# An attention kernel: latent queries as nine fp16 products instead of three fp32 ones, and the products moved between heads

## Chip, core and metric

One Trainium2 chip, one of its cores. The metric is the device time of one execution in microseconds, the median of the runs shown, with the lowest and the highest. The profile is of one further execution.

## What is computed

A two-layer block on x of shape (8, 256, 256) with a context of (8, 1601, 64). The change touches only the first attention of 16 heads:

```
q_big = einsum("bshk,hkq->bshq", (x_norm @ Wq.T) split in heads, w_kc_q)     # 192 wide
q_big = q_big * cos_q + rotate_half(q_big) * sin_q
q_r   = einsum("bshq,hqr->bhsr", q_big, W_qr)
k_r   = einsum("bld,hdr->bhlr", rope(kv_c), W_kr)
attn  = softmax(einsum("bhsr,bhlr->bhsl", q_r, k_r))
ctx   = einsum("bhsl,bld->bhsd", attn, rope(kv_c))
```

`W_qr` and `W_kr` are multiplied beforehand to a matrix M of 192 by 64 for each head. So the query of a head is first x times `w2` (192 wide), then rotated, then multiplied by M. The result, 64 wide, is the "latent query", which meets the rotated context directly.

## The kernel before

The program is written by hand in phases. In each, every engine has its own instruction list, and semaphores order them. A phase ends when all five lists have ended. No planner sets the order, it is the order of the code.

`phase_prepare` normalizes x, builds `w2` and M, rotates the context and writes the `w2` and M of each pair of heads to memory (`w2_scr`, `m_scr`). It ends some 76 us into the run.

`phase_attention0` runs 128 heads (8 batches of 16). After a start-up of some 30 us a loop of 32 rounds takes four heads a round. In a round u counts the heads 0 to 3. The queries are made for two heads at once, a pair p, and two heads ahead or more. This is spread over two heads of the loop:

- u even: `q_first` (12 fp16 matmuls of 256 columns into `psQ`, lines 747), VectorE then multiplies by sine (`turn_first`) and cosine (`cos_first`, in place in `psQ`), and adds (`add_first`, line 1039).
- u odd: `q_second` (6 fp16 matmuls), VectorE multiplies (1046, 1051) and adds (1055). Then `q_lat`: three fp32 matmuls with M (`ms`) on `roped` (line 772). ScalarE takes the top half of the result to fp16 (`q_high`, 942), VectorE the remainder (`q_low`, 1062), ScalarE copies the other half (`q_other`, 949).

Beside this every head has its own work. TensorE makes scores in four groups of key tiles (line 801), two in each of the PSUM tiles `psS[0]` and `psS[1]`. ScalarE takes the exponential (966). GpSimd makes the rest of the fp32 probability that bf16 leaves out (`rest_of`, 1178). TensorE multiplies both parts with the values (819, 822). For the head after the next TensorE makes eight "maxima" products of 400 columns (785) that alternate between the two banks of `psM`. VectorE reduces each (`reduce_max`, 1071). So the maximum k can start only when the reduction k-2 is done:

```
if not (isinstance(n, int) and n == 0 and k < ST):
    pe.wait_ge(mx_done, PASSES * n + k - 1)
```

The maxima of one head are joined, and a shift made of them is turned by TensorE (`shift`, line 789) and copied by ScalarE (954). GpSimd also adds up each head's output (`total`, 1184 and 1186). SyncE issues the loads of `w2` and M for the following pair.

## Time and profile before

| | us |
|---|---|
| median of 3 runs | 1658.73 |
| lowest, highest | 1655.77, 1659.28 |
| the profiled execution | 1660.06 |
| its span | 1658.1 |

| engine | busy us | share of the span |
|---|---|---|
| TensorE | 1589.3 | 96% |
| VectorE | 1305.9 | 79% |
| GpSimd | 1021.2 | 62% |
| ScalarE | 1013.7 | 61% |

Busy is the time in which an engine has at least one instruction under way. TensorE's instructions overlap: a matmul's length includes the way through the array, so the distance from one start to the next tells what it costs, not its length. An fp32 matmul stands in the trace as two records. In the 40 slices of the page the attention loop fills slices 3 to 27. The clock granted to TensorE is full there.

### The profile page before, as it was taken

The page shows a single profiled execution, that of the slowest core. Times are in us where ns is not written, and L with a number is a line of the kernel's source. Part 1 is how long each engine was busy: PE and PEld are TensorE (multiplying, and loading weights), DVE is VectorE, ACT ScalarE, POOL GpSimd, SP SyncE. Part 2 cuts the span into 40 slices and gives each one's busy share as a digit, 9 for nine tenths or more (in the row PEclk, how much of TensorE's full clock was granted, in tenths as well). Part 3 has the DMA queues.
Part 4 walks back from the last instruction along what each step waited for, and adds up shares of the span by engine and source line. Part 5 has one row for each costly group of instructions (what it writes and reads, how often), then busy time and mean ns, then how long its engine had stood idle before and what let it go on. Part 6 is the DMA issues. An engine that isn't in the chain of part 4 may idle for free. (4 is left out here: it accounts for less than half of the span.)

```text
span 1658.1 us, 48690 instructions
## 1 busy us (share of the span) xinstructions
PE 1589.3 (96%) x16127; PEld 1299.1 (78%) x16127; DVE 1305.9 (79%) x3044; ACT 1013.7 (61%) x2024; POOL 1021.2 (62%) x970
## 2 busy tenths in 40 slices
PE   5889999999999999999999999999899899999998
PEld 4668888888888888888888888888786445556787
DVE  6988888888888888888888888888783578885223
ACT  5876767676777676767676777676222466664121
POOL 5348888888888888888888888788100224431321
PEclk8699999999999999999999999999999999999999
DMA  9721121121122122112112114412940011101244
GB/s 257 252 78 44 51 78 44 46 83 46 45 72 59 40 65 63 47 51 79 40 54 79 43 51 112 86 44 81 219 85 0 7 42 65 65 8 53 100 148 160
DMA packets 184808, 125.97 MB, mean 76 GB/s; under 512 B 107562, under 2 KB 171992, under 8 KB 184368
## 3 DMA queue, kind: packets, MB, share of 16 engines
q1 hardware_dynamic: 183216, 121.27, 26.5%
q0 software_dynamic: 1536, 3.99, 0.7%
q8 instruction: 31, 0.51, 0.1%
q14 instruction: 25, 0.20, 0.0%
HBM read 81.98 MB, written 24.48 MB: 64 GB/s over the span
## 5 line engine op out<-in xcount | busy, mean ns | idle before, releaser
L1178 POOL TENSOR_TENSOR c_rest<-c_prob 128x1024 f16<-128x1024 f32 (+1 forms) x513 | 801.4, 1572 | 209.1 <-ACT c_prob L966 186.5
L1071 DVE TENSOR_REDUCE c_mxp<-c_psM 128x1 f32<-128x400 f32 (+1 forms) x1040 | 581.8, 572 | 98.1 <-PE c_psM L785 86.5
L966 ACT ACTIVATE c_prob<-c_psS,ln,c_exp_scale 128x1024 f32<-128x1024 f32 (+1 forms) x514 | 536.4, 1044 | 193.7 <-PE c_psS L801 188.7
L801 PE MATMUL c_psS<-c_q,c_kk 128*128 128x256 f16 (+1 forms) x3350 | 512.8, 272 | 0.1
L819 PE MATMUL c_psV<-c_vb,c_prob 128*128 128x129 f16 (+1 forms) x3328 | 428.8, 221 | 1.2 <-ACT c_acc L1020 1.2
L822 PE MATMUL c_psV<-c_vb,c_rest 128*128 128x65 f16 (+1 forms) x3328 | 401.0, 193 | 0.0
L801 PEld LDWEIGHTS c_psS<-c_q,c_kk 128*128 128x128 f16 (+1 forms) x3350 | 312.6, 99 | 69.1 <-issue 0.3
L785 PE MATMUL c_psM<-c_kkm,c_q 128*128 128x400 f16 (+1 forms) x1040 | 346.1, 333 | 4.4 <-DVE c_mxp L1071 3.0
L822 PEld LDWEIGHTS c_psV<-c_vb,c_rest 128*128 128x128 f16 (+1 forms) x3328 | 303.4, 98 | 33.4
L819 PEld LDWEIGHTS c_psV<-c_vb,c_prob 128*128 128x128 bf16 (+1 forms) x3328 | 313.6, 97 | 9.4 <-ACT c_acc L1020 1.4
L747 PE MATMUL c_psQ<-c_xb,c_w2s 128*128 128x256 f16 x1188 | 162.7, 274 | 6.9 <-PEq L163 4.8
L2141 ACT ACTIVATE g_prob<-g_psS,g_bias 128x128 f32<-128x128 f32 (+1 forms) x256 | 103.8, 426 | 49.8 <-DVE g_bias L2191 49.8
L747 PEld LDWEIGHTS c_psQ<-c_xb,c_w2s 128*128 128x128 f16 x1188 | 102.7, 97 | 23.5 <-issue 7.9
L785 PEld LDWEIGHTS c_psM<-c_kkm,c_q 128*128 128x128 f16 x1040 | 101.3, 97 | 13.7 <-DVE c_mxp L1071 4.6
L942 ACT ACTIVATE c_q<-c_psQ 64x256 f16<-64x256 f32 x132 | 49.8, 378 | 86.2 <-PE c_psQ L772 84.6
L772 PE MATMUL c_psQ<-c_roped,c_ms 128*128 128x256 f32 x396 | 101.5, 392 | 1.0 <-DVE c_roped L1055 1.0
L954 ACT ACTIVATE c_q<-c_psM 32x128 f16<-32x128 f16 x258 | 68.9, 267 | 34.3 <-PE c_psM L789 29.0
L1243 POOL TENSOR_SCALAR xn_rows<-x_rows,f_n_agg,f_n_rstd 128x256 f32<-128x256 f32 x3 | 3.9, 1316 | 127.1 <-DVEq L1260 127.1
L2596 DVE TENSOR_TENSOR m_g<-m_s,m_psH 128x256 f32<-128x256 f32 (+1 forms) x48 | 20.1, 420 | 78.7 <-ACT m_s L2543 66.1
L772 PEld LDWEIGHTS c_psQ<-c_roped,c_ms 128*128 128x128 f32 x396 | 69.9, 190 | 7.9 <-DVE c_roped L1055 1.1
L2198 DVE COPY g_pT<-g_psT 128x1024 f32<-128x1024 f32 x48 | 58.8, 1224 | 12.8 <-PE g_psT L2044 11.8
L2191 DVE TENSOR_REDUCE g_bias<-g_psS 128x4 f32<-128x1024 f32 (+1 forms) x48 | 58.7, 1223 | 11.8 <-PE g_psS L2035 7.5
(323 smaller groups left out, 2188.5 us busy)
## 6 DMA issues: line engine op xcount, KB each, us to landing
c_w2s<-w_scr SPq DMA_DIRECT2D x66, 256.0 KB, 2.6
c_ms<-m_scr SPq DMA_DIRECT2D x67, 192.0 KB, 2.3
c_w2s<-w_scr SPq DMA_DIRECT2D x66, 128.0 KB, 2.0
acc_scr<-c_acc SPq DMA_DIRECT2D x129, 64.0 KB
kv<-acc_scr SPq DMA_DIRECT2D x16, 512.0 KB, 6.6
m_w<-in_L_ffn_W SPq DMA_DIRECT2D x16, 352.0 KB, 3.5
c_vb<-V SPq DMA_DIRECT2D x27, 129.0 KB, 2.0
c_kk<-KK SPq DMA_DIRECT2D x27, 128.0 KB, 2.0
```

The lines of the kernel that those rows point to most:

```text
L747: mm = pe.matmul(out, weights[:, w, c], xb[:, x, c, :], start=(c == 0 and i == 0), stop=(c == DK - 1 and i == 2))
L772: mm = pe.matmul(psQ[:, S:2 * S], ms[:, e, :], roped[:, e, :], start=(e == 0), stop=(e == 2))
L785: pe.matmul(psM[:, st, 0:w], q1[slot][:, st * P:(st + 1) * P], kkm[:, c0:c0 + w], start=True, stop=True).then_inc(mx_full, 1)
L801: mm = pe.matmul(psS[g % 2][0:r, i * S:(i + 1) * S], src[:, (lo + i) * P:(lo + i) * P + r], mov[slot][:, :], start=(one == 0 and i % 2 == ...
L819: pe.matmul(psV[:, st * W:(st + 1) * W], high[0:r, c0:c0 + P], vb[0:r, i, :], start=(i == 0 and st == 0), stop=False, skip_group_check=True)
L822: mm = pe.matmul(psV[:, st * W + DC:(st + 1) * W], rest[g][0:r, c0:c0 + P], vb[0:r, i, DC:W], start=False, stop=(i == LT - 1), skip_group_ ...
L954: last = nc.scalar.activation(q2[slot][0:2 * SHIFT_ROWS, st * P:(st + 1) * P], shiftT[st * 2 * SHIFT_ROWS:(st + 1) * 2 * SHIFT_ROWS, :], A ...
L966: nc.scalar.activation(prob[g][0:r, 0:w], psS[g % 2][0:r, 0:w], ACT.Exp, bias=keep["ln1024"][0:r, :], scale=exp_scale[slot][0:r, :]).then_ ...
L1071: nc.vector.tensor_reduce(mxp[:, st, c:c + 1], psM[:, st, 0:CHUNKS[c][1]], AX.X, ALU.max).then_inc(mx_done, 1)
L1178: nc.gpsimd.tensor_tensor(rest[g][0:r, 0:w], prob[g][0:r, 0:w], high[0:r, 0:w], ALU.subtract).then_inc(rest_done, 1)
L2141: ins = nc.scalar.activation(prob[k % 2][:, i * w:(i + 1) * w], psS[k % 2][:, i * w:(i + 1) * w], ACT.Exp, bias=bias[k % 2][:, i:i + 1], a ...
L2198: nc.vector.tensor_copy(pT[k % 2][:], psT[:]).then_inc(pt_done, 1)
```

## The change

The latent query is made by nine fp16 matmuls. M and the rotated query are each split in a high and a low fp16 part: M high and M low times the high part of the query (`q_lat_high`, six), then M high times the low part (`q_lat_low`, three). ScalarE makes the high part (`rope_high`, two activations a pair, of 512 and 256 columns), GpSimd the low one (`rope_low`, two subtractions).

The order changes too. `q_second` is now in the even head and `q_first`, for the pair after, in the odd one, into the upper half of `psS[1]`. VectorE multiplies by cosine from there into a new tile `ropeA` in SBUF, and `add_first` adds `ropeA` and `ropeB`. `q_lat` comes in the odd head between the shift and the second half of the first values. `add_first` and `add_second` stand in the even head, between reductions. `q_low` stands right behind `cos_first` in the odd head, ahead of seven of the eight reductions.

In the preparation M is no longer scaled by one instruction. ScalarE writes the high part head by head (16), behind its copies of `woT`, VectorE the low one head by head (16), behind its last turn of the context. SyncE issues twelve stores instead of six, and the load of M moves to the attention. One of the turns of the context goes from VectorE to GpSimd. The activation that loads the table of the exponential moves from the end of the preparation into the start of the attention.

```diff
@@ phase_prepare, SyncE
-            sp.wait_ge(m_scaled, 1)
-            for e in range(2):
-                c0 = e * P
-                sp.dma_start(t["m_scr"][:, 0:HALF, c0:c0 + DC]...
-                sp.dma_start(t["m_scr"][:, HALF:P, c0 + DC:c0 + 2 * DC]...
-                sp.dma_start(t["m_scr"][:, e * REM:(e + 1) * REM, 2 * P + DC:PQ]...
-            sp.wait_ge(m_stored, 16 * 6)
-            sp.dma_start(keep["ms"][:], ...).then_inc(keep["in_m"], 16)
+            for part, ready in ((0, m_high), (1, m_low)):
+                sp.wait_ge(ready, H0)
+                for e in range(2):
+                    c0, c2 = (2 * e + part) * P, (4 + part) * P
...
@@ phase_prepare, GpSimd
             nc.gpsimd.partition_all_reduce(aall[:], amax[:], P, ...)
+            turn(POOL_TURNS, B - 1)
@@ phase_prepare, ScalarE
+            act.wait_ge(mscale_ready, 1)
+            for h in range(H0):
+                nc.scalar.activation(m2[:, 0, h, :, :], m[:, h, :, :], ACT.Copy,
+                                     scale=m_scale[0:HALF, h:h + 1]).then_inc(m_high, 1)
             act.wait_ge(m_cleared, 16)
...
-            nc.scalar.activation(warm[:], eps[:], ACT.Exp)
@@ phase_prepare, VectorE
-            nc.vector.tensor_tensor(
-                m[:], m[:], m_scale[0:HALF, :]...broadcast_to([HALF, H0, 2, DC]),
-                ALU.mult).then_inc(m_scaled, 1)
+            dve.sem_inc(mscale_ready, 1)
...
-            for b in range(POOL_TURNS + 1, B):
+            for b in range(POOL_TURNS + 1, B - 1):
                 turn_context(b)
+            for h in range(H0):
+                dve.wait_ge(m_high, h + 1)
+                nc.vector.scalar_tensor_tensor(out=m2[:, 1, h, :, :], in0=m[:, h, :, :], ...
@@ phase_attention0, TensorE, the loop
                     scores(n, 3, u)
+                    if u % 2 == 1:
+                        q_first(p + 1, 0, ahead_q)
                     values(n, 0, (0, 1))
-                    if u % 2 == 0:
-                        q_first(p, 0)
                     maxima(n + 2, p2, 0, s2)
-                    values(n, 0, (1, 2))
-                    if u % 2 == 0:
-                        q_first(p, 1, maxima_of=n + 1)
+                    if u % 2 == 1:
+                        q_first(p + 1, 1, ahead_q, maxima_of=n + 1)
+                        shift(n + 1)
+                        values(n, 0, (1, 2))
+                        q_lat_high(p)
+                        q_lat_low(p)
                     else:
+                        values(n, 0, (1, 2))
                         q_second(p, maxima_of=n + 1)
-                    shift(n + 1)
+                        shift(n + 1)
...
                     if u % 2 == 1:
-                        q_lat(p)
+                        pe.wait_ge(turnA, 3 * p + 6)
                     maxima(n + 2, p2, 4, s2)
@@ phase_attention0, ScalarE, the loop
-                    if u % 2 == 0:
-                        q_other((AHEAD // 2) * j + (u + 2) // 2, (u + 2) % AHEAD)
                     exp(n, 2, u)
...
+                    if u % 2 == 1:
+                        exp(n, 3, u)
+                        shift_copy(n + 1, (u + 1) % AHEAD)
+                        q_high(p, u - 1)
...
                     if u % 2 == 1:
-                        q_high((AHEAD // 2) * j + (AHEAD + u) // 2, u - 1)
+                        q_other(p, u - 1)
+                    else:
+                        rope_high(p, slice(0, 2), ropedA)
                     exp(n + 1, 1, (u + 1) % AHEAD)
...
+                    if u % 2 == 0:
+                        rope_high(p, slice(2, 3), ropedR)
@@ phase_attention0, VectorE
-                nc.vector.tensor_tensor(psQ[:], psQ[:], tabA[:, 0:2 * S], ALU.mult).then_inc(turnA, 1)
+                nc.vector.tensor_tensor(ropeA[:], src[:, 0:2 * S], tabA[:, 0:2 * S], ALU.mult).then_inc(turnA, 1)
...
-                nc.vector.tensor_tensor(roped[:, 0:2, :].rearrange("p e s -> p (e s)"), psQ[:],
+                nc.vector.tensor_tensor(roped[:, 0:2, :].rearrange("p e s -> p (e s)"), ropeA[:],
                                         ropeB[:, 0:2, :].rearrange("p e s -> p (e s)"), ALU.add)
@@ phase_attention0, GpSimd, the loop
                     rest_of(n + 1, 0)
+                    if u % 2 == 0:
+                        rope_low(p, slice(0, 2), 1)
+                        rope_low(p, slice(2, 3), 2)
```

Before, TensorE in an odd head around `q_lat`; `c_psQ<-c_roped,c_ms` is the product with M, `c_psM<-c_kkm` a maximum, here the fourth and the fifth of eight:

```order
L785 MATMUL c_psM<-c_kkm,c_q_1 128x400
L796 REGISTER_ALU
L801 MATMUL c_psS<-c_q_0,c_kk 128x256 x2
L819 MATMUL c_psV<-c_vb,c_prob 128x129
L822 MATMUL c_psV<-c_vb,c_rest 128x65
L819 MATMUL c_psV<-c_vb,c_prob 128x129
L822 MATMUL c_psV<-c_vb,c_rest 128x65
L772 MATMUL c_psQ<-c_roped,c_ms 128x256 x3
L783 REGISTER_ALU
L785 MATMUL c_psM<-c_kkm,c_q_1 128x400
L801 MATMUL c_psS<-c_q_0,c_kk 128x256 x4
```

After, TensorE in an odd head; line 769 is `q_first` for the following pair, 819 the shift, 849 and 852 the values, 795 and 801 the nine products:

```order
L769 MATMUL c_psS<-c_xb,c_w2s 128x256 x5
L768 ISA
L769 MATMUL c_psS<-c_xb,c_w2s 128x256
L819 MATMUL c_psM<-ident_sb,c_mcol 128x128
L849 MATMUL c_psV<-c_vb,c_prob 128x129
L852 MATMUL c_psV<-c_vb,c_rest 128x65
L849 MATMUL c_psV<-c_vb,c_prob 128x129
L852 MATMUL c_psV<-c_vb,c_rest 128x65
L791 REGISTER_ALU
L795 MATMUL c_psQ<-c_ropedH,c_ms 128x256 x6
L801 MATMUL c_psQ<-c_ropedL,c_ms 128x256 x3
L849 MATMUL c_psV<-c_vb,c_prob 128x129
```

The product with M has moved from its place between the fourth and the fifth maximum to one just behind the shift, ahead of the second maximum.

Before, VectorE in an odd head, between the sines of the second product (1046) and the fourth reduction:

```order
L1071 TENSOR_REDUCE c_mxp<-c_psM 128x1
L1046 TENSOR_TENSOR c_ropeB<-c_psQ,c_tabB 64x256 x2
L1051 TENSOR_TENSOR c_psQ<-c_psQ,c_tabA 128x256
L1067 REGISTER_ALU
L1071 TENSOR_REDUCE c_mxp<-c_psM 128x1
L1055 TENSOR_TENSOR c_roped<-c_psQ,c_ropeB 128x256
L1067 REGISTER_ALU
L1071 TENSOR_REDUCE c_mxp<-c_psM 128x1
```

After, VectorE in an odd head, from the first reduction on; `c_psS` is the half tile that `q_first` now writes, lines 1126 are `q_low`:

```order
L1136 TENSOR_REDUCE c_mxp<-c_psM 128x1
L1089 REGISTER_ALU
L1091 TENSOR_TENSOR c_ropeB<-c_psS,c_tabB 128x256 x2
L1095 TENSOR_TENSOR c_ropeA<-c_psS,c_tabA 128x512
L1123 ISA
L1126 SCALAR_TENSOR_TENSOR c_q_0<-c_psQ,c_q_0 64x256
L1126 SCALAR_TENSOR_TENSOR c_q_1<-c_psQ,c_q_1 64x256
L1132 REGISTER_ALU
L1136 TENSOR_REDUCE c_mxp<-c_psM 128x1
```

`q_low` (before: lines 1062, behind the sixth reduction) now stands ahead of the second one.

Before, VectorE in an even head around `add_first` (1039), behind the sixth reduction:

```order
L1071 TENSOR_REDUCE c_mxp<-c_psM 128x1
L1067 REGISTER_ALU
L1071 TENSOR_REDUCE c_mxp<-c_psM 128x1
L1038 REGISTER_ALU
L1039 TENSOR_TENSOR c_roped<-c_psQ,c_ropeB 128x512
L1067 REGISTER_ALU
L1069 ISA
L1071 TENSOR_REDUCE c_mxp<-c_psM 128x1
L1075 ISA
```

After, VectorE in an even head, where `add_first` (1101) and `add_second` (1119) now stand among the reductions:

```order
L1136 TENSOR_REDUCE c_mxp<-c_psM 128x1
L1098 REGISTER_ALU
L1100 ISA
L1101 TENSOR_TENSOR c_roped<-c_ropeA,c_ropeB 128x512
L1132 REGISTER_ALU
L1136 TENSOR_REDUCE c_mxp<-c_psM 128x1
L1119 TENSOR_TENSOR c_roped<-c_psQ,c_ropeB 128x256
```

Both inputs of `add_first` are now in SBUF, `c_ropeA` and `c_ropeB`; before one of them was `c_psQ`.

## Rows read from the trace of the kernel before

**Rows 1.** Busy time by stretch: window, length, engines with instruction counts, clock, DMA.

```profile
400.00:600.00 200.00, 200.00 (x2411) 173.50 (x2410) 174.42 (x413) 141.00 (x221) 163.93 (x146) 1.00 0.19 54
```

**Rows 2.** Timeline of TensorE in the loop: start us, length, line, tiles, shapes.

```profile
609.28 0.22 PE L819 MATMUL c_psV<-c_vb,c_prob 128*128 128x129 f16 x1
...
611.54 0.33 PE L785 MATMUL c_psM<-c_kkm,c_q 128*128 128x400 f16 x1
...
612.11 1.54 PE L772 MATMUL c_psQ<-c_roped,c_ms 128*128 128x256 f32 x6
613.48 0.33 PE L785 MATMUL c_psM<-c_kkm,c_q 128*128 128x400 f16 x1
...
615.00 0.33 PE L785 MATMUL c_psM<-c_kkm,c_q 128*128 128x401 f16 x1
...
616.17 0.60 PE L801 MATMUL c_psS<-c_q,c_kk 128*128 128x256 f16 x4
...
616.79 0.82 PE L747 MATMUL c_psQ<-c_xb,c_w2s 128*128 128x256 f16 x6
617.44 0.33 PE L785 MATMUL c_psM<-c_kkm,c_q 128*128 128x400 f16 x1
...
628.58 1.54 PE L772 MATMUL c_psQ<-c_roped,c_ms 128*128 128x256 f32 x6
```

**Rows 3.** Timeline of ScalarE, the same stretch.

```profile
613.68 0.78 ACT L942 ACTIVATE c_q<-c_psQ 64x256 f16<-64x256 f32 x2 [1.26 <-PE c_psQ L772]
```

**Rows 4.** Timeline of VectorE, the same stretch.

```profile
611.68 1.05 DVE L1071 TENSOR_REDUCE c_mxp<-c_psM 128x1 f32<-128x400 f32 x2
...
615.06 0.88 DVE L1062 TENSOR_TENSOR c_q<-c_psQ,c_q 64x256 f16<-64x256 f32 x2
615.97 0.57 DVE L1071 TENSOR_REDUCE c_mxp<-c_psM 128x1 f32<-128x401 f32 x1
...
622.79 0.68 DVE L1039 TENSOR_TENSOR c_roped<-c_psQ,c_ropeB 128x512 f32<-128x512 f32 x1
```

**Rows 5.** Timeline of GpSimd, the same stretch.

```profile
611.92 0.46 POOL L1184 TENSOR_TENSOR c_acc<-c_acc 128x128 f32<-128x128 f32 x1
612.32 0.18 POOL L1186 COPY kv<-c_acc 128x2 f32 x1
612.63 1.89 POOL L1178 TENSOR_TENSOR c_rest<-c_prob 128x1024 f16<-128x1024 f32 x1
```

**Rows 6.** Timelines of VectorE and GpSimd in the preparation.

```profile
21.96 0.97 DVE L77 TENSOR_TENSOR a_tmp<-a_rstd 128x16 f32<-128x16 f32 x1
22.96 0.18 DVE L78 SCALAR_TENSOR_TENSOR a_tmp<-a_agg,a_tmp 128x16 f32<-128x16 f32 x1
23.17 1.81 DVE L79 TENSOR_SCALAR a_tmp<-a_tmp 128x16 f32<-128x16 f32 x1
...
21.83 1.07 POOL L247 TENSOR_TENSOR a_rot<-kv,a_sink 128x416 f32<-128x416 f32 x1
22.97 1.98 POOL L251 TENSOR_TENSOR kv<-kv,a_cosk 128x832 f32<-128x832 f32 x1
```

**Rows 7.** Timelines at the end of the preparation: ScalarE, SyncE, VectorE, then TensorE.

```profile
66.01 2.56 ACT L397 ACTIVATE a_x<-a_psA 128x512 f32<-128x512 f32 x5 [0.21 <-PE a_psA L327]
...
71.98 1.28 ACT L408 ACT_TABLE_LOAD   x1
...
68.43 0.36 SPq L223 DMA_DIRECT2D m_scr<-a_m  x1
...
71.59 0.62 SPq L227 DMA_DIRECT2D m_scr<-a_m  x1
...
74.26 1.02 DVE L442 TENSOR_TENSOR kv<-kv,a_rot 128x832 f32<-128x832 f32 x1
...
76.12 2.72 PE L747 MATMUL c_psQ<-c_xb,c_w2s 128*128 128x256 f16 x12 [4.80 <-PEq L163]
```

**Rows 8.** ScalarE by line and shape in the preparation: busy us, mean ns.

```profile
L366 ACT ACTIVATE a_wqk<-a_w,a_w_scale 128x128 f16<-128x128 f32 x8 | 3.2, 395 | 0.0
```

More of the change, by code:

```diff
@@ L240, in _, with turn @@
             h, r = DC // 2, rot[0]
-            for b in range(POOL_TURNS):
+            def turn(i, b):
                 pool.wait_ge(in_k[b], 32)
-                if b >= 1:
-                    pool.wait_ge(roped, b)
+                if i >= 1:
+                    pool.wait_ge(roped, i)
                 nc.gpsimd.tensor_tensor(r[:, :, 0:h], kv[:, b, :, h:DC], sink[:, :, 0:h],
@@ L764, in q_second, with q_lat_high, q_lat_low @@
                 pe.wait_ge(in_wR, 16 * (p + 1))
-                pe.wait_ge(ropedA, p + 1)
+                pe.wait_ge(turnA, 3 * p + 3)
+                if not isinstance(p, int) or p > 0:
+                    pe.wait_ge(ropedR, p)
+                    pe.wait_ge(ql_done, 2 * p)
                 q_rows(psQ[:, 0:S], wR, maxima_of).then_inc(qR_full, 1)
-            def q_lat(p):
-                pe.wait_ge(ropedR, p + 1)
+            def q_lat_high(p):
+                pe.wait_ge(rh_done, 2 * p + 2)
                 pe.wait_ge(in_m, 16 * (p + 1))
                 for e in range(3):
-                    mm = pe.matmul(psQ[:, S:2 * S], ms[:, e, :], roped[:, e, :], start=(e == 0), stop=(e == 2))
+                    for part in range(2):
+                        pe.matmul(psQ[:, S:2 * S], msp[:, e, part, :], ropedH[:, e, :],
+                                  start=(e == 0 and part == 0), stop=False, skip_group_check=True)
+            def q_lat_low(p):
+                pe.wait_ge(rl_done, 2 * p + 2)
+                for e in range(3):
+                    mm = pe.matmul(psQ[:, S:2 * S], msp[:, e, 0, :], ropedL[:, e, :],
+                                   start=False, stop=(e == 2), skip_group_check=True)
                 mm.then_inc(qk_full, 1)
@@ L936, in _, with rope_high @@
         def _(act):
+            def rope_high(p, blocks, ready):
+                act.wait_ge(ready, p + 1)
+                if not isinstance(p, int) or p > 0:
+                    act.wait_ge(qk_full, p)
+                nc.scalar.activation(ropedH[:, blocks, :], roped[:, blocks, :], ACT.Copy).then_inc(rh_done, 1)
             def q_high(p, slot):
@@ L941, in q_high @@
                     rows = slice(u * DC, (u + 1) * DC)
[L942 removed]
+                    nc.scalar.activation(q1[slot + u][rows, :], psQ[rows, S:2 * S], ACT.Copy,
+                                         scale=1.0 / M_UP).then_inc(qh_done, 1)
             def q_other(p, slot):
@@ L986, in _ @@
             v_top(4)
+            rope_high(0, slice(0, 2), ropedA)
             keys_copy(2)
+            rope_high(0, slice(2, 3), ropedR)
             keys_copy(3)
+            nc.scalar.activation(warm[:], keep["ln1024"][:], ACT.Exp)
             q_high(0, 0)
```

162 lines of the change are left out of this document (101 added, 61 removed).

## The prediction, made before the changed kernel was run

> **What bounds the kernel now.** Read the busy time by stretch first [rows 1]: in 200 us of the attention loop TensorE is busy for all 200, at the full clock (1.00, the 2.4 GHz level). VectorE has 174.42 and GpSimd 163.93. Then the timeline of TensorE [rows 2]. It shows one pair of heads: from one product with M (612.11) to the next (628.58) are 16.47 us, without an idle stretch named. So in the loop each column that TensorE is spared is time won, and each wait that it gets is time lost, 64 times. What must be read next is therefore who comes just in time for TensorE: the reductions, the halves of the query, and GpSimd, whose rows [rows 3 to 5] give the margins. Last the end of the preparation [rows 7], where not TensorE but the last list to end decides.
>
> All sums are changes to the profiled execution (1660.06, span 1658.1). Its own distance to the median is 1.3 us, and the changes are then put on the median, 1658.7.
>
> **The product itself.** Three fp32 matmuls with M hold TensorE from 612.11 to 613.48, 1.37 us [rows 2]. Six fp16 matmuls of the same 256 columns take from 616.79 to 617.44, 0.65 us, 0.108 each. Nine take 0.975. The gain is 0.395 us a pair, in 64 pairs 25.3 us. That is the most the change can bring in the loop, since nothing else leaves TensorE there. The other halves of the query are only moved.
>
> **The wait that the move makes, odd head.** Call the start of the nine products 0. The last one starts at 0.87 and ends at 1.14 (the six of [rows 2] end 0.82 after the first start). ScalarE followed 0.03 after the product's end at 613.65 [rows 3], so `q_high` runs from 1.17, for 0.78: till 1.95. `q_low` starts at 2.00 and costs VectorE 0.91 until the next reduction (615.06 to 615.97) [rows 4]: 2.91. Only now comes the second reduction, 0.57 long: 3.48. The fourth maximum waits for it and can start at 3.53. TensorE gets there earlier: 0.975 for the nine, then the values, scores and maxima that stood between 609.28 and 611.54 [rows 2], 2.26 us. That is 3.24. **TensorE waits 0.30 us.** If the new form of `q_low` (scaled subtraction) costs 0.06 more each, 0.42. I take 0.35, times 64 is 22.4 us. Before, `q_low` stood behind the sixth reduction and held nobody. The second half of the score tile is clear by then (`cos_first` ends about 1.5 after 0), so the new wait on `turnA` costs nothing. ScalarE is free for `q_high`: the exponential ahead of it and the shift's copy are done by about 0.7.
>
> **The even head.** TensorE's order is that of the old odd head without the product with M, so those rows serve as its clock. The fourth maximum is at 611.54 and ends 0.33 to 0.37 later, the fourth reduction starts at 611.91, and VectorE steps on every 0.49 (two reductions in 1.05) [rows 4]. So `add_first` comes at 612.40. Its two inputs are both in SBUF now. GpSimd at that time ends its sum (611.92, 0.46), copies (612.32 to 612.50) and starts the next big subtraction at 612.63 [rows 5].
>
> Here the trace has a warning, in the preparation [rows 6]. A VectorE operation on 16 columns with two inputs in SBUF (line 77) took 0.97 us and ended at 22.93, right behind GpSimd's operation (to 22.90). Line 78, of the same size, started 0.01 ahead of GpSimd's next one and took 0.18. Line 79 came 0.2 later and took 1.81, until GpSimd was done at 24.95. So who comes second waits for the whole of the other. The Trainium skill says it in "SBUF — State Buffer", section "Who interferes with whom": a VectorE instruction with two SBUF inputs and a GpSimd one that reads SBUF exclude each other for the instruction's length. The trace agrees, with the 0.97 against 0.18.
>
> For `add_first` this gives: it comes during the copy, waits 0.1, runs 612.50 to 613.18 (0.68 for 512 columns [rows 4]). GpSimd's subtraction starts at 613.2 rather than 612.63. The fifth reduction ends about 613.67, the seventh maximum wants to start at 615.00 less 1.37, 613.63: wait 0.08. `rope_high` (512 columns) stands ahead of an exponential on ScalarE, from 613.2 for 0.7, and the exponential (1.2) ends about 615.05. The next head's last scores need it at 616.17 less 1.37 plus 0.22, 615.02: wait 0.1. Together 0.2 us a pair (0 to 0.4), 12.8 us. The half tile of GpSimd's delay is covered: its values are wanted 0.7 us later than it was done. GpSimd as a whole gets two subtractions of 768 columns together (1.89 for 1024 gives 1.4, and 0.46 for 128 shows a fixed part, so 1.6 to 2.0) and some 0.6 of blocking onto 13.4 of 16.4 us. It stays a little below the pair's length and isn't the bound, but it has no slack left.
>
> Loop: -25.3 + 22.4 + 12.8 = **+9.9 us** (-6 to +25).
>
> **The preparation.** Its end is set by the last list: VectorE at 75.28 (74.26 + 1.02), and TensorE starts 0.84 later, at 76.12 [rows 7]. VectorE is relieved of the scaling and one turn, and gets 16 small operations. But SyncE becomes the last. Six stores took from 68.43 to 72.21, 0.63 each; twelve are 7.6 us, and they start only when all 16 high parts are there. ScalarE's copies ahead end at 68.57 (66.01 + 2.56). A scaled copy of 128 columns takes 0.395 [rows 8], overlapped about 0.3: 16 are 4.7 us. Without any other delay that is 73.3, and SyncE ends at 80.9: +5.6. GpSimd's extra turn (four operations of 1.07 to 1.98 as in [rows 6]) now runs beside VectorE's chain of small operations for the scale, and each with two SBUF inputs may wait for one of them. I count 1.1 us more on ScalarE's start. So +6.7 us (+3, if stores of half the bytes issue faster, to +9). The load of the table (1.28, 71.98) was hidden behind VectorE there.
>
> **The start of the attention.** The table load and its activation, 1.5 us, now stand ahead of the first `q_high`, which all else waits for; some 0.5 of it was idle: +1.0. One `q_first` more is made in all, 1.3 us. Two products with M are cheaper, -0.8. The low parts on GpSimd and VectorE's remainders of V (two SBUF inputs) get in each other's way, +0.5 to +1. Together +2.5 us (+1 to +4).
>
> **Sum.** 9.9 + 6.7 + 2.5 = +19.1. On the median 1658.7: **1678 us**, 1.2% slower.
>
> **The rivals.**
> - *The gain is kept.* If `q_high` and `q_low` follow each other faster than I chain them, TensorE never waits: -25.3 + 5.6 + 1 = -18.7, 1640 us. Against it stands that each link of the 3.53 is a row. For it, that some waits in the even head are near zero. 0.12, faster.
> - *A wash.* The odd wait is the 0.30 of the rows, the even head is free: -6.1 + 5.6 + 1.3, 1659.5. 0.14, within 0.2%.
> - *`add_first` is caught.* It comes 0.23 us ahead of GpSimd's big subtraction (612.40 against 612.63). If it comes behind, it waits until 614.52, runs 0.68, the fifth reduction ends at 615.69 and TensorE stands at the seventh maximum for 2.1 us instead of 0.08. In all 64 pairs that is +129, some 1807 us. It decides at a shift of 0.23 us between the two. The rule of the skill named above gives just this. 0.09, slower; caught in some rounds only, or GpSimd as the bound, another 0.05, 1705 to 1760.
> - My forecast, 1664 to 1697, has 0.60.
>
> About 0.2% is what a measurement of this kernel can tell from no change, here 3.3 us. Faster by more: 0.12. Within: 0.14. Slower: 0.74. The range goes from 1655 to 1705: my case with the bounds of its terms, and the wash.
>
> **What the profile will show.** The nine products at a distance of 0.108, 0.975 in all. Right behind them ScalarE, then `q_low`, and the fourth maximum of odd heads with idle time released by the reduction, 0.3 to 0.4 us, 64 times. If that idle time is missing, the step is wrong and the loop is faster. In even heads `add_first` should take 0.7 to 0.8 with its wait; 2 us would be the caught case. The first matmul of the attention should start near 83 rather than at 76.12, with SyncE's last store just ahead of it. A pair should take about 16.6 us. The forecast fails if the stores issue far faster than 0.63, or if TensorE's waits in both heads add to less than 0.4.

## The result, and the profile after

| | before | after |
|---|---|---|
| median, us | 1657.76 | 1662.88 |
| lowest, highest | 1655.77, 1659.28 | 1660.72, 1663.38 |
| profiled span | 1658.1 | 1661.1 |

The ratio of after to before is **1.0024, with a 95% interval of 1.0016 to 1.0033**: slower by some 4 us. The forecast was 1678, 19 us more than the 1658.7 before. The direction and the range held. The size did not: about four fifths of the loss that was forecast are not there. It also fell between two of the bands that had a chance of their own, "within 0.2%" and 1664 to 1697. Each ratio in this document is to executions of the kernel before that were taken beside the kernel in question, so times of different kernels are compared by their ratios.

Where the time went is read first from marks that both kernels have. TensorE's first attention matmul is at 76.12 before [rows 7] and here after (timeline of TensorE):

```profile
84.36 2.72 PE L769 MATMUL c_psQ<-c_xb,c_w2s 128*128 128x256 f16 x12 [11.77 <-PEq L165]
```

The second mark is the shift matmul of head 1, the first of the loop (108.44 and 118.16). The third is ScalarE's last copy of an accumulator (1160.00 and 1164.09). That gives three stretches:

| stretch | before | after | change | forecast |
|---|---|---|---|---|
| preparation, to 76.12 / 84.36 | 76.12 | 84.36 | +8.2 | +6.7 |
| start of the attention, to the loop's first shift | 32.32 | 33.80 | +1.5 | +2.5 |
| loop, to the last copy | 1051.56 | 1045.93 | **-5.6** | +9.9 |
| all | | | +4.1 | +19.1 |

In the second row 0.65 us of the work with the query stands on the other side of the mark after the change (`q_second` ahead of that shift instead of both halves of `q_first`). Put back it reads +2.1 and -6.3. So the sign of the whole comes from the preparation and the start alone: the loop, which was forecast as the larger part of the loss, got faster. Behind the third mark the distance between the kernels drifts from +3.8 (where VectorE starts on the next normalisation, 1299.3 and 1303.1) over +5.2 (1341.6 and 1346.8) to +3.0 at the end, in code that the change does not touch. That is scatter of single executions. So is part of the 84.36: in the five further kernels here that have the same preparation (a1, a2, a3, c1 and f1 below) the mark lies at 83.24 to 84.15.

The loop is what the forecast missed. A pair of heads, counted between the first `q_high` and the last one in 140 to 1000 us, lasts 16.44 us before (16.41 and 16.47 in turn) and 16.36 after (16.32 and 16.38). Forecast were 16.6. The stretch of [rows 1] after the change:

```profile
400.00:600.00 200.00, 198.53 (x2458) 171.63 (x2457) 174.49 (x419) 149.99 (x246) 190.61 (x172) 1.00 0.19 53
```

TensorE, busy for all 200 before, now has holes, at the same full clock (1.00, the 2.4 GHz level). GpSimd went from 163.93 to 190.61. The busy times of the whole span, from the page of after:

```profile
PE 1575.7 (95%) x16337; PEld 1284.3 (77%) x16337; DVE 1306.2 (79%) x3058; ACT 1062.0 (64%) x2174; POOL 1160.3 (70%) x1106
```

TensorE is busy for 14 us less than before and the span is longer all the same.

Now the odd head, TensorE's timeline (start us, length, line, tiles):

```profile
649.65 0.82 PE L795 MATMUL c_psQ<-c_ropedH,c_ms 128*128 128x256 f16 x6
650.31 0.49 PE L801 MATMUL c_psQ<-c_ropedL,c_ms 128*128 128x256 f16 x3
...
652.38 0.33 PE L815 MATMUL c_psM<-c_kkm,c_q 128*128 128x400 f16 x1
...
653.19 0.34 PE L815 MATMUL c_psM<-c_kkm,c_q 128*128 128x400 f16 x1
```

and ScalarE's and VectorE's beside it:

```profile
650.84 0.78 ACT L990 ACTIVATE c_q<-c_psQ 64x256 f16<-64x256 f32 x2 [0.61 <-PE c_psQ L801]
```

```profile
651.65 0.88 DVE L1126 SCALAR_TENSOR_TENSOR c_q<-c_psQ,c_q 64x256 f16<-64x256 f32 x2 [0.67 <-ACT c_q L990]
652.55 2.75 DVE L1136 TENSOR_REDUCE c_mxp<-c_psM 128x1 f32<-128x400 f32 x5
```

The nine products take 0.98 (649.65 to 650.63, where the values begin). `q_high`, `q_low` and the reductions follow one another as the chain of the forecast had them, and the fourth maximum stands at 653.19 where the values end at 652.90: 0.29 us. The list of waits of 130 to 1150 us (engine, line, for whom: us in total, times, longest) has this wait, and for TensorE no other that counts:

```profile
PEld c_psM L815 <- DVE c_mxp L1136: 16.8, 62, 0.3
```

Of the even head the forecast took 0.2 us of waits. VectorE there (`add_first`, then the fifth reduction), then GpSimd, ScalarE (`rope_high`, then the exponential behind it) and TensorE's seventh maximum:

```profile
644.92 0.68 DVE L1101 TENSOR_TENSOR c_roped<-c_ropeA,c_ropeB 128x512 f32<-128x512 f32 x1
645.53 0.56 DVE L1136 TENSOR_REDUCE c_mxp<-c_psM 128x1 f32<-128x400 f32 x1
```

```profile
644.52 0.45 POOL L1260 TENSOR_TENSOR c_acc<-c_acc 128x128 f32<-128x128 f32 x1
644.92 0.73 POOL L1262 COPY kv<-c_acc 128x2 f32 x1
645.61 1.89 POOL L1246 TENSOR_TENSOR c_rest<-c_prob 128x1024 f16<-128x1024 f32 x1
```

```profile
645.72 0.63 ACT L983 ACTIVATE c_ropedH<-c_roped 128x512 f16<-128x512 f32 x1 [0.80 <-DVE c_roped L1101]
646.25 1.19 ACT L1015 ACTIVATE c_prob<-c_psS,ln,c_exp_scale 128x1024 f32<-128x1024 f32 x1
```

```profile
646.15 0.34 PE L815 MATMUL c_psM<-c_kkm,c_q 128*128 128x401 f16 x1
```

`add_first` came at its forecast place (0.87 behind the fourth maximum at 644.05, forecast 0.86) and did not wait. The copy did: 0.73 us where [rows 5] have 0.18. The two met, but the one that was held was GpSimd, which has time for it. This head is one of only 4 of 49 between 200 and 1000 us. In the others the copy is over just in time and it is the big subtraction that is held, 2.2 us or a little more instead of 1.89, as one pair of heads later:

```profile
661.25 0.68 DVE L1101 TENSOR_TENSOR c_roped<-c_ropeA,c_ropeB 128x512 f32<-128x512 f32 x1
```

```profile
661.16 0.18 POOL L1262 COPY kv<-c_acc 128x2 f32 x1
661.49 2.19 POOL L1246 TENSOR_TENSOR c_rest<-c_prob 128x1024 f16<-128x1024 f32 x1
```

`add_first` takes 0.679 to 0.702 us in all 49, also where it began 0.09 behind the copy's start. It is 0.24 ahead of the subtraction (forecast 0.23). Counted from the fourth maximum, the fifth reduction ends at 2.04 (forecast 2.13), and the seventh maximum starts at 2.10, where it was wanted at 2.09. The exponential behind `rope_high` ends at 3.39 (forecast 3.51), before the 3.48 at which the scores want it. So neither of the two waits is there.

### The profile page after: what moved, and what is told of

Read it like the earlier page. It is cut to its first block and busy times, and to the rows that moved or that the text cites. A ratio compares the mean times of both kernels' runs of the same rounds, so it can differ in the third digit from the quotient of the medians.

```text
span 1661.1 us, 50090 instructions
## 1 busy us (share of the span) xinstructions
PE 1575.7 (95%) x16337; PEld 1284.3 (77%) x16337; DVE 1306.2 (79%) x3058; ACT 1062.0 (64%) x2174; POOL 1160.3 (70%) x1106
## 5 line engine op out<-in xcount | busy, mean ns | idle before, releaser
L1246 POOL TENSOR_TENSOR c_rest<-c_prob 128x1024 f16<-128x1024 f32 (+1 forms) x513 | 817.4, 1609 | 55.3 <-ACT c_prob L1015 34.7
L1015 ACT ACTIVATE c_prob<-c_psS,ln,c_exp_scale 128x1024 f32<-128x1024 f32 (+1 forms) x514 | 528.3, 1040 | 163.4 <-PE c_psS L831 161.7
L1136 DVE TENSOR_REDUCE c_mxp<-c_psM 128x1 f32<-128x400 f32 (+1 forms) x1040 | 572.1, 571 | 65.7 <-PE c_psM L815 49.8
L1254 POOL TENSOR_TENSOR c_ropedL<-c_roped,c_ropedH 128x512 f16<-128x512 f32 (+1 forms) x132 | 118.1, 912 | 18.5 <-ACT c_ropedH L983 18.5
L769 PE MATMUL c_psS<-c_xb,c_w2s 128*128 128x256 f16 x768 | 104.7, 273 | 0.0
L983 ACT ACTIVATE c_ropedH<-c_roped 128x512 f16<-128x512 f32 (+1 forms) x132 | 68.9, 522 | 48.6 <-DVE c_roped L1101 48.3
L1126 DVE SCALAR_TENSOR_TENSOR c_q<-c_psQ,c_q 64x256 f16<-64x256 f32 x132 | 55.8, 423 | 45.2 <-ACT c_q L990 43.1
L769 PEld LDWEIGHTS c_psS<-c_xb,c_w2s 128*128 128x128 f16 x768 | 73.2, 98 | 12.8
L769 PE MATMUL c_psQ<-c_xb,c_w2s 128*128 128x256 f16 x420 | 58.3, 277 | 12.7 <-PEq L165 11.8
```

What stands on the lines that cost most here:

```text
L769: mm = pe.matmul(out, weights[:, w, c], xb[:, x, c, :], start=(c == 0 and i == 0), stop=(c == DK - 1 and i == 2))
L983: nc.scalar.activation(ropedH[:, blocks, :], roped[:, blocks, :], ACT.Copy).then_inc(rh_done, 1)
L1015: nc.scalar.activation(prob[g][0:r, 0:w], psS[g % 2][0:r, 0:w], ACT.Exp, bias=keep["ln1024"][0:r, :], scale=exp_scale[slot][0:r, :]).then_ ...
L1136: nc.vector.tensor_reduce(mxp[:, st, c:c + 1], psM[:, st, 0:CHUNKS[c][1]], AX.X, ALU.max).then_inc(mx_done, 1)
L1246: nc.gpsimd.tensor_tensor(rest[g][0:r, 0:w], prob[g][0:r, 0:w], high[0:r, 0:w], ALU.subtract).then_inc(rest_done, 1)
L1254: nc.gpsimd.tensor_tensor(ropedL[:, blocks, :], roped[:, blocks, :], ropedH[:, blocks, :], ALU.subtract).then_inc(rl_done, 1)
```

## The experiments

All are the changed kernel with one edit, unless said otherwise. Where no part of the computation is named as left out, none is.

### The place of q_low in the odd head, three ways

**a1_low_behind_sixth.** `q_low` where it stood before the change.

```
                         cos_first(ahead_q)
-                        q_low(p, u - 1)
...
                     reduce_max(n + 2, 5)
+                    if u % 2 == 1:
+                        q_low(p, u - 1)
                     reduce_max(n + 2, 6)
```

> In odd heads q_low goes from ahead of the second reduction to behind the sixth; nothing else. Theory A (the fourth maximum of odd heads waits 0.29 us because q_low stands ahead of the second reduction, and nobody else is late): the wait of TensorE's weight load for the reduction, 16.8 us in 62 waits, falls to under 3 us, a pair goes from 16.355 to 16.07-16.12 us, the attention loop gains 15 to 18 us, and the time is about 1646 us, ratio to the kernel before 0.992-0.994. Rival B (VectorE's list as a whole is what the odd head lasts, so that q_low costs the same wherever it stands): the wait moves to a later maximum or to the shift of the next even head, the pair stays above 16.3, the time within 0.2% of 1663.

**a2_low_behind_second.** The same call behind `reduce_max(n + 2, 1)` of odd heads.

> In odd heads q_low goes behind the second reduction (one place later than in the changed kernel). A check of the ladder by which the wait was worked out: maximum k may start when reduction k-2 is done. The second maximum ends 652.10, so the second reduction would run to about 652.65, q_low 652.65-653.56, the third reduction to 654.13, while the fifth maximum wants to start at 653.47. Theory A: the wait of 0.29 at the fourth maximum disappears and one of 0.6-0.7 at the fifth takes its place; the pair lasts 16.7, about +0.35 or +22 us on the changed kernel, 1685 us. Rival B (VectorE's whole list decides, not the place): the same time as the changed kernel, 1663 within 4.

**c1_halves.** One half at each of two places.

```
                         cos_first(ahead_q)
-                        q_low(p, u - 1)
+                        q_low(p, u - 1, (0,))
...
                     reduce_max(n + 2, 5)
+                    if u % 2 == 1:
+                        q_low(p, u - 1, (1,))
                     reduce_max(n + 2, 6)
```

> q_low of odd heads is split: its first half (0.43 us) stays ahead of the second reduction, its second goes behind the sixth, where VectorE was idle for 0.52 us in the changed kernel. Three places have been timed whole: ahead of the second reduction 16.36 us a pair, behind the second 16.89, behind the sixth 16.33. Theory A (each place costs only what does not fit into its gap: ahead of the second reduction 0.43 fits and 0.88 not, behind the sixth 0.52 fits and 0.88 not): no wait at the fourth maximum and none at the next head's shift, a pair of 16.06-16.11, about -0.27 or -17 us on the changed kernel, 1645 us, ratio to the kernel before 0.992. Rival B (the odd head is bound by the sum of VectorE's list, so the same total costs the same): 16.3 a pair, ratio 1.000-1.002.

| | pair, us | ratio to before | 95% interval |
|---|---|---|---|
| changed kernel | 16.36 | 1.0024 | 1.0016 to 1.0033 |
| a1, behind the sixth | 16.33 | 1.0008 | 0.9999 to 1.0017 |
| a2, behind the second | 16.89 | 1.0226 | 1.0211 to 1.0242 |
| c1, halves | 16.09 | 0.9925 | 0.9911 to 0.9939 |

a1 made theory A fall as it was stated. The wait at the fourth maximum is gone, but only 0.03 us of the 0.29 are won. Its list of waits shows the new one, at the next even head, where the last matmul of `q_second`, right ahead of the shift, waits until VectorE has joined the maxima:

```profile
PEld c_psQ L769 <- DVE c_mcol L1153: 20.5, 57, 0.4
```

`q_second` takes 0.91 there from its start to the shift (655.30 to 656.21) instead of 0.65, which is the 0.26 that a1 does not win. The rival as it was stated, that `q_low` costs the same wherever it stands, falls by a2, whose pair is 0.54 longer.

a2 confirms the ladder (maximum k waits for reduction k-2) with the wait at the fifth maximum. It is 49.3 us in 61 waits at the weight load, 0.81 each, against 0.6 to 0.7 expected. Less the 0.27 of the changed kernel (16.8 in 62) that is 0.54, and the pair grew by 0.54, where 0.35 was expected. TensorE's timeline (the 0.66 in brackets is shorter, since it counts from the end of the matmul before):

```profile
655.40 0.34 PE L815 MATMUL c_psM<-c_kkm,c_q 128*128 128x400 f16 x1 [0.66 <-DVE c_mxp L1136]
```

The three places say: what counts is the gap at the place. Ahead of the second reduction VectorE waits for the maximum anyway, and half a `q_low` fits in. Behind the sixth it was idle for 0.52 us, and again a half fits and a whole (0.88) does not. c1 was worked out from that, and its VectorE shows both halves without a wait behind them:

```profile
642.79 0.42 DVE L1126 SCALAR_TENSOR_TENSOR c_q<-c_psQ,c_q 64x256 f16<-64x256 f32 x1 [0.68 <-ACT c_q L990]
643.28 2.87 DVE L1136 TENSOR_REDUCE c_mxp<-c_psM 128x1 f32<-128x400 f32 x5
646.18 0.43 DVE L1126 SCALAR_TENSOR_TENSOR c_q<-c_psQ,c_q 64x256 f16<-64x256 f32 x1
646.67 0.58 DVE L1136 TENSOR_REDUCE c_mxp<-c_psM 128x1 f32<-128x401 f32 x1
```

Neither wait of TensorE is left in its list, and TensorE is busy for 200.00 of 200 us again. Of the 0.395 that the products are shorter, the pair keeps 0.35 in the mean. Most pairs last 16.03 and 16.08 in turn, 0.385 less than before. The rest is lost at the changes of context, where one pair takes 16.22 to 16.84 and the list has the values waiting for GpSimd (`c_rest`, 5 waits at the weight load). So the new format brings what the column count says, and the wait of 0.29 in the changed kernel is the price of one undivided `q_low`. No run has the nine products at the old place, so what the format alone would do there is not shown.

### The even head: add_first behind GpSimd's start

**a3_add_behind_fifth.**

```
+                    reduce_max(n + 2, 4)
                     if u % 2 == 0:
                         add_first(p)
-                    reduce_max(n + 2, 4)
```

> In even heads add_first goes from ahead of the fifth reduction to behind it, 0.57 us later, so that it comes about 0.3 us behind the start of GpSimd's big subtraction instead of ahead of it. Theory A (who of VectorE and GpSimd comes second waits for the whole instruction of the other when VectorE has two inputs in SBUF): add_first waits some 1.5 us until GpSimd's 1.89 us subtraction is over, lasts above 2 us in the trace with the wait, the last maximum of the even head waits about 1.4 us, and the pair is 1.3 to 1.9 us longer: 85 to 120 us more than the changed kernel, 1750-1785 us. Rival B (in the loop it is always GpSimd that is held, as its copy of 0.73 us instead of 0.18 at 644.92 suggests): add_first stays at 0.68 us, GpSimd's subtraction becomes 0.5 longer, the time is within 5 us of the changed kernel.

Ratio **1.0756** (1.074 to 1.0772), 121 us more than the changed kernel, just past theory A's 85 to 120. A pair is 18.26, +1.90. VectorE, GpSimd and TensorE in one even head:

```profile
650.67 2.12 DVE L1101 TENSOR_TENSOR c_roped<-c_ropeA,c_ropeB 128x512 f32<-128x512 f32 x1
```

```profile
650.35 1.89 POOL L1246 TENSOR_TENSOR c_rest<-c_prob 128x1024 f16<-128x1024 f32 x1
```

```profile
653.66 0.34 PE L815 MATMUL c_psM<-c_kkm,c_q 128*128 128x401 f16 x1 [1.16 <-DVE c_mxp L1136]
...
654.60 0.41 PE L831 MATMUL c_psS<-c_q,c_kk 128*65 128x256 f16 x2 [0.37 <-ACT c_prob L1015]
```

`add_first` came 0.32 us behind GpSimd's start and ended 0.55 behind GpSimd's end at 652.24: it had waited for all of it, in every one of the 44 records between 200 and 1000 us:

```profile
L1101 DVE TENSOR_TENSOR c_roped<-c_ropeA,c_ropeB x44: 2050/2084/2118, 212.6 to 997.6; 128x512 f32<-128x512 f32 x44
```

(ns, least, median, greatest; in the changed kernel 679, 681 and 702.) The rival of the prediction, +129 us, was therefore real and priced right. It did not come about, since `add_first` begins 0.24 ahead of the subtraction. The maximum waited 1.16 and the scores of the next head another 0.37, because the exponential stood behind `rope_high`. Both brackets count from the end of the matmul before. From start to start TensorE lost more: its six scores from 651.68, at 0.109 each, are through at 652.33, and the maximum starts 1.33 later. The two scores behind it are followed by the next after 0.54. Together that is 1.87 of the 1.90.

### The preparation

What the changed kernel shows there. VectorE (with the sixteen low parts as the last row), then the same low parts as a group, then GpSimd, then SyncE's last stores:

```profile
68.53 1.97 DVE L451 TENSOR_TENSOR kv<-kv,a_cosk 128x832 f32<-128x832 f32 x1
70.53 1.79 DVE L452 TENSOR_TENSOR kv<-kv,a_rot 128x832 f32<-128x832 f32 x1
72.35 7.60 DVE L517 SCALAR_TENSOR_TENSOR a_rT<-a_m,a_m_scale,a_rT 96x128 f16<-96x128 f32 x16
```

```profile
L517 DVE SCALAR_TENSOR_TENSOR a_rT<-a_m,a_m_scale,a_rT x16: 335/336/2086, 72.4 to 79.6; 96x128 f16<-96x128 f32 x16
```

```profile
68.54 1.07 POOL L248 TENSOR_TENSOR a_rot<-kv,a_sink 128x416 f32<-128x416 f32 x1 [7.04 <-issue]
...
74.19 1.94 POOL L256 TENSOR_TENSOR kv<-kv,a_rot 128x832 f32<-128x832 f32 x1
```

```profile
77.43 0.62 SPq L231 DMA_DIRECT2D m_scr<-a_rT  x1
79.98 0.32 SPq L227 DMA_DIRECT2D m_scr<-a_rT  x1
...
82.78 0.58 SPq L231 DMA_DIRECT2D m_scr<-a_rT  x1
```

SyncE issues six stores, waits 1.9 us for the low parts, and issues the other six at 0.56 each (the first at 0.60). The low parts are late because VectorE shares 68.5 to 76.1 with GpSimd: products of 1.02 [rows 7] take 1.97 and 1.79, and two of the low parts about 2 us instead of 0.34. What GpSimd's extra turn did not do is disturb the chain of the scale, as the forecast had it: it began only at 68.54, when the chain was over.

**b1_turn_on_vector.** `turn(POOL_TURNS, B - 1)` is taken from GpSimd, and VectorE's loop goes to `B` again.

> The rotation of the last context goes back from GpSimd to VectorE in the preparation; the rest is the changed kernel. Theory A (the preparation is long because VectorE's operations with two SBUF inputs wait for whole GpSimd instructions: the products at 68.53 and 70.53 took 1.97 and 1.79 instead of 1.02, two of the 16 low parts 1.91 and 2.09 instead of 0.34): two turns of 3.25 us end at 73.9, the 16 low parts take 0.25 us each and end at 78.0-78.5, the last six stores end at 82.0, and TensorE's first attention matmul comes at 82.5-83.2 instead of 84.36 (83.6 to 84.4 in five runs); about 1 us less, ratio about 1.001-1.002. Rival B (a turn more on VectorE costs what it costs, the low parts are slow by themselves): low parts until 81 or later, start at 85 or later.

**b2_lows_first.**

```
+            for h in range(H0):
+                dve.wait_ge(m_high, h + 1)
+                nc.vector.scalar_tensor_tensor(...).then_inc(m_low, 1)
             for b in range(POOL_TURNS + 1, B - 1):
                 turn_context(b)
-            for h in range(H0):
...
```

> The changed kernel with VectorE's last two pieces of the preparation exchanged: the 16 low parts of M come ahead of the turn of context 6; GpSimd keeps its turn from 68.5 to 76.1. Theory A (exclusion): while GpSimd works on its four instructions, VectorE gets few low parts done per GpSimd instruction, several of them take 1 to 2.6 us, the low parts end behind 76, the turn adds 3.25 us, and TensorE's first attention matmul is not earlier than 83. Rival B (only the order on VectorE delays the stores): the low parts follow the high ones at 0.3 us and end at 75, SyncE issues all twelve stores in one row from 74.4 to 81.7, and TensorE starts at 82.5.

**b3_two_queues.** b1, and the stores of low parts with e = 1 are issued by ScalarE behind its last copy.

> As b1_turn_on_vector (last turn on VectorE), and of the six stores of low parts three are issued by ScalarE, which is idle there, beside SyncE's other three. Theory A (the end of the preparation is the issue of stores, 0.60 us each on one queue): the low parts end at 78.0-78.5 as in b1, the stores 1.8 us later, TensorE's first attention matmul at 80.5-81.3, 1.8 us ahead of b1; ratio 1.000-1.001. Rival B (the stores' transfer or the barrier at the block's end decides, not their issue): the start within 0.5 of b1.

| | TensorE's start | first q_high, behind it | shift of head 0, behind it | ratio | 95% interval |
|---|---|---|---|---|---|
| before | 76.12 | 9.56 | 22.29 | 1 | |
| changed kernel | 84.36 | 10.29 | 22.53 | 1.0024 | 1.0016 to 1.0033 |
| b1 | 81.92 | 13.52 | 28.19 | 1.0045 | 1.0029 to 1.006 |
| b2 | 82.57 | 10.41 | 22.71 | 1.0018 | 1.0009 to 1.0028 |
| b3 | 80.69 | 13.31 | 26.27 | 1.0035 | 1.0023 to 1.0048 |

In b1 no low part takes over 0.348 us, all sixteen are done in 4.29, and the start is 1.3 to 2.4 earlier than in the changed kernel and the five with the same preparation. The contention is shown, a little larger than expected (0.8 to 1.9). b2 is mixed. The low parts did crawl: from 69.37 to 74.7 each of GpSimd's last three instructions let one of them by (1.25, 2.09 and 2.09 us), and they ended at 78.06 and not at 75. The start of 82.57 is rival B's number all the same, but not by its path: SyncE had issued the first six stores by 77.31 and waited 0.78 for the low parts, where it waits 1.4 to 2.6 in the kernels with the other order. Twelve stores in one row would have been about 0.8 us earlier still (an estimate from this wait). The issue of the stores is the other part of the cost, and b3 shows it: on two queues the start is 1.2 earlier.

And yet b1 and b3 are no faster than the changed kernel. Their starts are earlier, but the first shift comes 3.7 to 5.7 us later behind it. GpSimd in b1:

```profile
92.75 1.77 POOL L1253 TENSOR_TENSOR c_ropedL<-c_roped,c_ropedH 128x512 f16<-128x512 f32 x2 [7.42 <-issue]
```

7.42 us pass between GpSimd's last memset and its first product of the attention, of which 4.3 after its input from ScalarE was there (88.48), and the first `q_high` is 3.2 us late with it. The changed kernel has the same 7.04 ahead of its extra turn, where they only delay the turn. So the turn on GpSimd was a good exchange for a reason that neither the diff nor the forecast names. These 3.2 us are not all of b1's 5.7. Another 1.2 are the twelve matmuls of the next `q_first`, 2.66 us where the changed kernel has 1.47: from 90 to 100 us the granted clock is 0.50 in b1 (the 1.2 GHz level), after TensorE had been busy for 1.13 of the 3 us before. And 0.9 are one remainder of V on VectorE (103.53), which began 0.01 behind a GpSimd product and took 2.02 instead of 1.08.

**e1_small_product.** b1, with one product of 4 columns on GpSimd behind the all-reduce.

```
             nc.gpsimd.partition_all_reduce(...).then_inc(aall_ready, 1)
+            nc.gpsimd.tensor_tensor(r[:, 0, 0:4], cosk[:, 0, 0:4], cosk[:, 0, 0:4],
+                                    ALU.mult).then_inc(rotated, 1)
```

> b1_turn_on_vector with one tiny GpSimd product of 4 columns right behind the all-reduce (its result is used by nobody). b1's attention began at 81.92, 1.8 us earlier than the changed kernel's, but lost 5.7 us by the first shift, because GpSimd's first product behind the all-reduce waited 7.42 us for its issue in the attention; in the changed kernel that wait (7.04 us) lies in the preparation, ahead of the extra turn. Theory A (GpSimd pays about 7 us once, at its first product behind the all-reduce, wherever that is): the tiny product pays it at 61-69 us, TensorE's start stays at 81.9, the first q_high comes 10.3 behind it and the first shift 22.5 (13.5 and 28.2 in b1); 5.6 us less than b1, ratio to the kernel before 1.000-1.002. Rival B (the 7.4 us belong to the attention's own block, or to the memsets ahead): entry as in b1, ratio 1.004.

```profile
68.74 0.19 POOL L264 TENSOR_TENSOR a_rot<-a_cosk 128x4 f32<-128x4 f32 x1 [7.04 <-issue]
```

The wait moved to the small product. Start 81.97, first `q_high` 10.29 behind it as expected, ratio 1.0019 (1.0009 to 1.0028). The first shift came 23.84 behind the start rather than 22.5. Of this 1.3 us the trace shows the place, the twelve matmuls of `q_first`. Here e1, then the changed kernel:

```profile
94.40 2.77 PE L769 MATMUL c_psQ<-c_xb,c_w2s 128*128 128x256 f16 x12
```

```profile
96.78 1.47 PE L769 MATMUL c_psQ<-c_xb,c_w2s 128*128 128x256 f16 x12
```

The granted clock of 92 to 104 us is 0.86 in e1, 1.00 in the changed kernel's 94 to 106. It is not that it came back late: it was 1.00 over 88 to 94, 0.50 (the 1.2 GHz level) over 94.40 to 97.80, just the twelve matmuls, and 1.00 again over 97.90 to 106. a2, with another edit altogether, has the same 0.86 and the same 23.87. In c1 the clock is 0.50 over 101.30 to 104.50, behind those matmuls, and the first shift stays at 22.53. Ahead of the matmuls TensorE had been idle for 1.54 us in e1 and for 1.53 in the changed kernel, and for 10.2 to 12.6 us ahead of the start in these kernels. Why the clock fell in some and not in others stays open.

**a4_table_early.** The activation `warm` goes from ahead of the first `q_high` back to the end of ScalarE's preparation.

> The load of the exponential's table (1.28 us with its activation's issue) goes from ahead of the first q_high back to the end of ScalarE's list in the preparation, where ScalarE is idle for 8 us. Theory A (my step: it delays the first q_high and all behind it): the distance from TensorE's first attention matmul to the first q_high falls from 10.29 to about 9.3, and to the first shift matmul from 22.53 by 0 to 0.8; time -0.5 us, not measurable in the ratio. Rival B (VectorE's list of reductions and remainders sets the first shift): q_high comes 1 us earlier, the shift matmul stays at 22.5.

First `q_high` 9.89 behind the start (10.29), shift of head 0 22.26 (22.53), ratio 1.0023 (1.0014 to 1.0032). The load costs 0.4 at the one and 0.3 at the other: theory A's sign, with less than half its size for the first `q_high`.

### Together

**e2_best** has c1, e1, the two queues of b3 and a4.

> All that helped, together: q_low of odd heads in halves (c1_halves), the last turn on VectorE with the tiny GpSimd product (e1), the stores of low parts on two queues (b3), the exponential's table loaded in the preparation (a4). Theory A (these are separate stretches, so their gains add): start of the attention at 80.4-80.9 instead of 83.2 in c1_halves, first shift 22.2-22.4 behind it, a pair of 16.09 us; c1_halves less 2.6 to 3.4 us: about 1647 us, ratio to the kernel before 0.990-0.9915. Rival B (an earlier start only moves waits, as in b1): not below c1_halves, ratio 0.9925.

Ratio 0.9908 (0.9891 to 0.9925), a pair of 16.08, but a start at 81.83. ScalarE's timeline names the cause, the table load behind the stores:

```profile
78.46 0.94 ACTq L177 DMA_DIRECT2D m_scr<-a_rT  x1
79.74 1.28 ACT L425 ACT_TABLE_LOAD   x1 [4.48 <-issue]
```

**e3_table_ahead** exchanges the two.

> e2_best with the exponential's table loaded ahead of ScalarE's three stores instead of behind them. In e2_best the stores kept ScalarE's list until 79.40, the table load stood behind them (79.74 to 81.23), and TensorE began at 81.83 instead of the 80.69 of b3. Theory A (the table load had become the last of all lists): it moves to about 75.3, the start comes at 80.5-80.9, 1.1 us earlier than e2_best, too little for the ratio (0.990). Rival B (the landing of the stores decides): the start stays at 81.8.

Start 80.64, as theory A had it, **ratio 0.9903** (0.9887 to 0.992). That is some 16 us faster than the kernel before. It is the lowest ratio of a complete version here, but its interval overlaps those of e2 and of c1 alone (0.9911 to 0.9939). Most of the gain is c1's. What the preparation adds to it is seen in the marks, and is too small for the ratio to show.

**f1_six_products** is c1 with the three products of the low part left out, so the latent query lacks its smallest term.

```
-                for e in range(3):
-                    mm = pe.matmul(psQ[:, S:2 * S], msp[:, e, 0, :], ropedL[:, e, :], ...)
-                mm.then_inc(qk_full, 1)
```

> c1_halves with six products of M instead of nine: the three with the low part of the rotated query are left out, so the latent query lacks its smallest term. What is the loop's bound once the odd head's wait is gone? Theory A (TensorE: each product's 0.108 us counts): a pair falls by 0.325, from 16.09 to 15.75-15.80, 21 us less than c1_halves. Rival B (GpSimd, 193.69 of 200 us busy in c1_halves, which is 15.58 us a pair and 99% of a pair of 15.77): the pair stays above 15.85, TensorE shows waits for c_rest or GpSimd has no idle time left.

Ratio 0.9809 (0.9793 to 0.9826). Pairs of 15.70 and 15.75, 0.33 less than in c1: theory A for most of them. But at each change of context one pair takes 16.31 to 16.54, 0.56 to 0.79 more than its neighbours, where c1 loses 0.14 to 0.76, and the mean is 15.81. GpSimd's share suggests why such a pair is not made good:

```profile
400.00:600.00 200.00, 199.59 (x2509) 172.47 (x2506) 181.96 (x434) 154.91 (x253) 196.41 (x178) 1.00 0.19 54
```

With 196.41 of 200 us GpSimd has little time left to catch up after it waited for the new values (`c_vb`, 8 waits), and its `c_rest` keeps TensorE's values waiting 14 times. So it looks to be next behind TensorE. No run relieved it, so this is argued and not shown.

## Why the prediction was right and wrong

- **What bounds the kernel** was right. In the loop, TensorE's columns and waits add up to the pair: 16.44 less 0.395 plus 0.29 is 16.34, measured 16.36.
- **The product**, 0.975 us against 1.37: measured 0.98. Right, and c1 kept 0.35 of the 0.395.
- **The wait of the odd head** was right in place, chain and releaser. The rows gave 0.30, and 0.29 was measured. The 0.35 that was taken added a price for the new form of `q_low` that does not exist: 0.423 us, as the old one. That makes 3.8 of the 15.5 us by which the loop was missed.
- **The even head is the step that failed**: 0.2 us a pair, 12.8 us, where the pair leaves 0.02 (16.36 against 16.34), 1 us in all. It was made of three differences of 0.1 or less between rows of two decimals, each rounded to a loss. The first had the wrong side: that `add_first` waits 0.1 for GpSimd's copy. It was GpSimd that waited, and GpSimd had the time. With that 0.1 gone the wait of 0.08 at the seventh maximum is gone too. The third, 0.1 at the next head's scores, was reckoned with 1.85 us from the start of `rope_high` to the end of the exponential. Measured were 1.72, since `rope_high` takes 0.63 rather than 0.7 and the exponential starts 0.10 before it ends. The +9.9 for the loop should have been -25.3 + 19 + 1, about -5. That is the loop of the "wash" among the rivals, which had 0.14 and gave 1659.5.
- **The direction** was right by luck as far as the loop goes: it was forecast to lose 9.9 us and won 5.6. The kernel is slower because of the preparation and the start, +9.7 together where +9.2 was forecast.
- **`add_first` caught** at 0.09: did not happen, but a3 showed the mechanism, and its price (+121 us against 129) when `add_first` comes 0.57 later. The lead of 0.24 that saved it was forecast as 0.23. That the exclusion holds for the whole of the other's instruction is what the Trainium skill says in "SBUF — State Buffer", section "Who interferes with whom", and the traces agree (2.08 against 0.68). Where `add_first` overlaps the copy, 0.18 long, no hold of `add_first` is seen.
- **The preparation**: +6.7 forecast, +8.2 measured (+7.1 to +8.0 in the kernels with the same preparation). SyncE as the last list was right, and its stores took 0.60 and 0.56 rather than 0.63. The 1.1 us of contention had the right culprit and the wrong victim: not the chain of the scale, but VectorE's turn and the low parts, which then held SyncE for 1.9 us. ScalarE's high parts did begin 1.0 us behind the 68.57 of the forecast (69.60), but not by contention with GpSimd's turn, which had hardly begun (68.54). ScalarE's copies ahead of them wait for TensorE, and the place of the high parts goes roughly with its granted clock: that clock over 66 to 69 us was 0.72 in this execution and 1.00 in the kernel before; with 0.91 in a1 and 0.82 in c1 the high parts began at 68.68 and 68.56, with 0.58 in f1 at 69.88.
- **The start of the attention**: +2.5 forecast, +1.5 (+2.1 with the work moved across the mark). Right in sum. Of its terms, the table load was +0.4 rather than +1.0.

## What to carry to other kernels

Where an engine is bound and others step in time with it, what a piece of work costs is what does not fit into the gap at its place: look for two gaps of half the length before moving the whole piece, and see behind the wait you remove for the one that comes next. Do not add several waits of a tenth that each come from rounding. They are as likely zero, and multiplied by the loop they carried this forecast off. A list in the preparation may do a service that its rows only show elsewhere, so read the start of the next stage as well, when you take something off an engine.

## What was not expected of the hardware

- GpSimd's first product behind its all-reduce comes 6.9 to 7.4 us late, with no releaser in the profile, wherever it was put here: 7.04 us in the changed kernel, 7.42 in b1 in the middle of the attention's start, 7.04 in e1 for a product of 4 columns. Memsets in between (81.58 in b1) do not pay it. The all-reduce itself has 7.10 ahead of it in the kernel before. What happens in that time no trace shows.
- When VectorE and GpSimd alternate on SBUF, small VectorE operations come through one for each GpSimd instruction: three low parts in 5.3 us in b2, where by themselves one starts every 0.26.
- The granted clock at the start of the attention was 0.86 in some executions and 1.00 in others over the same 12 us, with the same preparation in a2 and the changed kernel. A stretch at 0.50 cost 1.3 us at the first shift where it met the twelve matmuls of `q_first` (e1, a2) and nothing where it came behind them (c1).
